# Attention and a mixture of experts on one core: the fills between the first 40 dispatch scatters write 560 elements instead of 200

## The chip, the core and the metric

The kernel runs on one core of one Trainium2 chip, in one launch. The metric is the device time of an execution in microseconds, lower being better. The kernel before has a median of 341.74 us over three runs (339.79, 341.74 and 344.94 us).

## What is computed

The input x has 8 batches of 512 rows of 128 numbers, all float32. The layer is causal attention with one head, a layer norm, a mixture of 8 experts of which each row takes 2, and two more layer norms. Cut to what matters:

```python
x = layernorm(x + softmax(mask(x Wq (x Wk)^T / sqrt(128))) (x Wv))
logits = (x @ gate_w + gate_b) / 0.9
keep = the two largest of the 8 logits of each row
gate = softmax of those two
h = gelu(x @ w1[e] + b1[e])            # 128 -> 512, for each kept expert e
y = sum over the two e of gate[e] * (h @ w2[e] + b2[e])
out = layernorm(x + (layernorm(y) * ln_g + ln_b))
```

## The kernel before

The work is cut into tiles of 128 rows: 4 tiles (TB) a batch, 32 in all. It has two stages that overlap a little.

**Attention and routing** go batch by batch (B = 8). In `step(b)` of each engine, TensorE transposes the next batch's rows, multiplies, transposes the probabilities and weighs the values; VectorE takes the row maxima (`maxima`, L732), adds the residual (L742) and computes the norms; ScalarE takes the exponentials and copies results out of the accumulators (among them v, L586). Two batches behind, VectorE turns the two chosen experts of each row into a place in a table in HBM: `route_link`, whose last link (L840) increments `dispatch_ready`. After the fifth batch, `table_link` also computes which expert each tile of the table belongs to. The table is divided into two groups of batches, `GROUPS = (5, 3)`, and each group's part by expert.

**Dispatch.** GpSimd writes each batch's rows to their places: 8 indirect DMAs (scatters) a batch, one for each of its 4 tiles and each of the 2 choices, 128 rows of 130 numbers each (L1129). Ahead of each scatter stands a fill, `pause(n)` (L1122): GpSimd writes zeros to a tile on one partition that nobody reads, and waits for its own semaphore `paused` before it goes on. There are 64 scatters, 40 of them for the first five batches. Only when all scatters of a group have landed (`dispatched[g]`) may SyncE load tiles of that group: for group 0 this wait stands in SyncE's order behind the copies of rows of batches 0 to 6 (L247) and the fill of the pads (L250), and ahead of the first loads of slots (L276).

**Experts.** 78 tiles of 128 table rows (J = 47 + 31), in loops of 8. For each tile SyncE loads the slots, TensorE transposes them (L510), VectorE copies the transposed tile out (`copy_slots`, L918), TensorE multiplies with the expert's first matrix (L525), ScalarE applies gelu (L668) and copies the expert's weights for a later tile (L661), TensorE multiplies with the second matrix (L536), VectorE weighs the result (L926), and GpSimd scatters it back to row order (`give_back`, L1136), again with a fill ahead of it (for all but the last four). TensorE holds three tiles between a tile's first and second product (LAG = 3).

The last batch's norm and routing stand in VectorE's order ahead of its first `copy_slots`; the places of batch 6 are computed just behind the first two copies, and those of batch 7 within the first eight tiles (at s = 5 and 6). GpSimd's order is: dispatch of batches 0 to 6, three returned tiles, dispatch of batch 7, the other returns. When the returns are in, the last layer norms follow by VectorE and ScalarE.

The order of every engine is written out by hand; no scheduler decides it. Waits are on semaphores alone.

Of the kernel before, what the change touches and what calls it, by code (L numbers as in the profile page):

```python
# [16 lines left out]
GROUPS = (5, 3)  # L17
# [1 line left out]
LAG = 3  # L19
W1_LAG = 3  # L20
AHEAD = 2
PAUSE = 200
TEMPERATURE = 0.9
EPS = 1e-5
BSCALE = 64.0
# [4 lines left out]
def moe_block(nc, emb, W_Q, W_K, W_V, gate_w, gate_b, w1, b1, w2, b2, ln_g, ln_b, out):  # L30
    B, S, D = emb.shape
    E, _, F = w1.shape
    TB = S // P
# [3 lines left out]
    TOPK = 2  # L37
# [25 lines left out]
    with ctx:  # L63
        def sb(name, shape, dt=F32):
            return ctx.enter_context(nc.sbuf_tensor(name, shape, dt))

        def sem(name):
            return ctx.enter_context(nc.semaphore(name))
# [5 lines left out]
        ones_h = sb("ones_h", [P, P], F16)  # L74
        ones = sb("ones", [P, E])
        unused = sb("unused", [P, 1])
        pause_out = sb("pause_out", [1, PAUSE])
        expert_id = sb("expert_id", [P, E])
        first_place = sb("first_place", [P, G, E])
        tile_start = sb("tile_start", [1, MOST_TILES])  # L80
# [996 lines left out]
        def _(pool):  # L1077
            made = sem("made")
            paused = sem("paused")
            g_ = nc.gpsimd  # L1080
# [36 lines left out]

            RETURNS_AHEAD = 3

            def pause(n):  # L1120

                g_.memset(pause_out[:], 0.0).then_inc(paused, 1)  # L1122
                pool.wait_ge(paused, n)

            def dispatch(b, t):
                for k in range(TOPK):
                    pause((b * TB + t) * TOPK + k + 1 + (RETURNS_AHEAD if b == B - 1 else 0))
                    c = k * TB + t
                    g_.indirect_dma_start(slots, bass.IndirectOffsetOnAxis(ap=slot_of[:, b, c:c + 1], axis=0),  # L1129
                                          rows[:, k, b * TB + t, :], None).then_inc(dispatched[0 if b < group_b0[1] else 1], 16)  # L1130

            def give_back(j):
                if j < J - 4:
                    pause(NT * TOPK + j + 1 if j >= RETURNS_AHEAD else NT * TOPK - TB * TOPK + j + 1)
                pool.wait_ge(y_ready, j + 1)
                g_.indirect_dma_start(returned, bass.IndirectOffsetOnAxis(ap=slot_back[:, j:j + 1], axis=0),  # L1136
                                      y[:, j % Y_RING, :], None).then_inc(y_returned[j % Y_RING], 16)
# [6 lines left out]
            for b in range(B):  # L1144
                if b == B - 1:
                    for j in range(RETURNS_AHEAD):
                        give_back(j)
                pool.wait_ge(dispatch_ready, b + 1)
                pool.wait_ge(rows_copied[b], 16)
                for t in range(TB):  # L1150
                    dispatch(b, t)
# [29 lines left out]
```

## Time and profile before

| | |
|---|---|
| median of three runs | 341.74 us (339.79 to 344.94) |
| the profiled execution's own time | 345.1 us |
| its span, first to last instruction | 343.2 us |
| TensorE busy | 264.2 us, 77% |
| VectorE busy | 184.4 us, 54% |
| ScalarE busy | 196.4 us, 57% |
| GpSimd busy | 185.3 us, 54% |
| granted TensorE clock, mean | 0.899 of full speed |
| fills of 200 elements (L1122) | 138, 254 ns each |
| dispatch scatters (L1129) | 64, 976 ns each |
| return scatters (L1136) | 78, 976 ns each |

Busy shares are averages over stages that are limited by different things, so they say little about a change in one stage. The chain of waits follows the work that ended last back to what released it at each step; "issue" is time in which an engine waited for nothing that the profile shows, and "another core or an unknown queue" or "remote" is a wait whose end cannot be matched with the end of an instruction. The timeline gives for each instruction its start, how long it took, how long its engine stood idle before it and what ended that. GpSimd is POOL there, VectorE DVE, ScalarE ACT, TensorE PE (matmuls) and PEld (loads of weights), SyncE SP.

### The profile page before, as it was taken

Reading aid. Unit: us, or ns where it says so; the run is one execution under the profiler, and the core shown is the slowest. Engines: PE = TensorE matmul, PEld = TensorE weight load, DVE = VectorE, ACT = ScalarE, POOL = GpSimd, SP = SyncE. Lnnn points to the kernel's source line nnn. Section 1 sums busy time; section 2 is a strip of 40 time slices with the busy share of each in tenths; the row PEclk is TensorE's granted clock in tenths of the full one; section 3 lists DMA queues with packets and bytes.
Section 4 is the critical chain, followed back from the end, with each engine's and each line's share of the span. In section 5 each row is a group of like instructions: output and inputs, shape, how many; then the busy total and the mean of one; then the engine's idle time right before and its main releaser. Section 6 shows DMA issues by size and latency. Waiting matters only on the chain.

```text
span 343.2 us, 8076 instructions
## 1 busy us (share of the span) xinstructions
PE 264.2 (77%) x1993; PEld 234.2 (68%) x1994; DVE 184.4 (54%) x990; ACT 196.4 (57%) x579; POOL 185.3 (54%) x310
## 2 busy tenths in 40 slices
PE   3998887796863658787799999999999999950000
PEld 2567666485643557686799999999999999950000
DVE  0225783756766643332343333466348878862785
ACT  3357663474533454643568787755555688854251
POOL 8200078766884668678755565656556546560200
PEclk9999999699995869997699999999999999995555
DMA  5996022121232343232212324667699565017403
GB/s 140 273 332 165 8 64 79 39 71 39 72 100 71 76 119 81 56 78 55 64 56 81 96 78 125 179 182 216 193 357 317 179 176 164 31 40 205 140 0 93
DMA packets 45634, 41.94 MB, mean 122 GB/s; under 512 B 5520, under 2 KB 36416, under 8 KB 45600
## 3 DMA queue, kind: packets, MB, share of 16 engines
q1 hardware_dynamic: 41056, 32.20, 33.4%
q0 software_dynamic: 4544, 9.38, 8.0%
q14 instruction: 24, 0.20, 0.2%
q8 instruction: 10, 0.16, 0.2%
HBM read 26.00 MB, written 13.47 MB: 115 GB/s over the span
## 4 chain that ended last, share of the span: by engine, by line
PE 49%; DVE 22%; issue 7%; another core or an unknown queue 7%; DVEq 5%; ACT 5%; DMA 2%; POOL 1%; SPq 1%; ACTq 0%
PE bank L536 15%; PE bank L525 13%; PE bank L425 4%; PE bank L398 4%; DVE sum_stats L931 3%; PE bank L384 2%; DVEq L973 2%; DVE negmax L732 2%; PE bank L389 2%; PE bank L510 2%; PE bank L413 2%; DVE x L926 2%; DVE slot_xT L918 1%; PE bank L533 1%
## 5 line engine op out<-in xcount | busy, mean ns | idle before, releaser
L668 ACT ACTIVATE h<-bank,b_cols 128x128 f32<-128x128 f32 x312 | 89.5, 373 | 51.6 <-PE bank L525 36.7
L1136 POOL DMA_INDIRECT returned<-x,slot_back x78 | 76.1, 976 | 61.8 <-DVE x L926 34.6
L536 PE MATMUL bank<-w_all,h 128*128 x624 | 90.6, 289 | 0.8 <-issue 0.7
L525 PE MATMUL bank<-slot_xT,w_now 128*128 128x128 f32 x624 | 86.0, 282 | 3.3 <-ACT h L668 2.0
L525 PEld LDWEIGHTS bank<-slot_xT,w_now 128*128 128x128 f32 x624 | 79.1, 198 | 4.7 <-issue 3.4
L536 PEld LDWEIGHTS bank<-w_all,h 128*128 128x128 f32 x624 | 78.4, 197 | 2.1 <-issue 1.0
L1129 POOL DMA_INDIRECT slots<-rows,slot_of x64 | 62.5, 976 | 17.8 <-issue 13.9
L1122 POOL MEMSET pause_out<- 1x200 f32 x138 | 35.1, 254 | 44.8 <-DVE rows L840 44.2
L926 DVE TENSOR_SCALAR x<-bank,slot_gate 128x128 f32<-128x128 f32 x78 | 27.1, 348 | 42.7 <-PE bank L536 23.0
L678 ACT ACTIVATE pair<-pair,sum_shift,sum_rstd 128x128 f32<-128x128 f32 x60 | 25.2, 492 | 22.8 <-DVE sum_shift L949 18.8
L661 ACT ACTIVATE w_now<-w_all 128x512 f32 x40 | 26.0, 651 | 7.5 <-issue 7.5
L916 DVE CAST slot_back<-slot_x 128x1 uint32<-128x1 f32 x78 | 11.7, 149 | 32.8 <-PE bank L510 22.4
L732 DVE TENSOR_REDUCE negmax<-bank 128x1 f32<-128x128 f32 (+3 forms) x32 | 15.0, 489 | 24.1 <-PE bank L399 18.6
L425 PE MATMUL bank<-v,probsT 128*128 128x128 f32 x160 | 24.6, 297 | 3.9 <-ACT probsT L595 2.7
L510 PE MATMUL bank<-ident,slot_x 128*128 128x128 f32 x78 | 22.3, 286 | 6.0 <-DVE slot_xT L918 4.0
L425 PEld LDWEIGHTS bank<-v,probsT 128*128 128x128 f32 x160 | 21.4, 205 | 6.2 <-ACT probsT L595 4.4
L608 ACT ACTIVATE probs<-bank,negmax 128x128 f32<-128x128 f32 (+3 forms) x32 | 16.6, 525 | 11.5 <-DVE negmax L732 8.2
L398 PE MATMUL bank<-xT,gT 128*128 128x128 f32 (+3 forms) x64 | 22.6, 477 | 0.0
L595 ACT ACTIVATE probsT<-bank 128x384 f32<-128x384 f32 (+1 forms) x24 | 12.0, 528 | 18.0 <-PE bank L413 13.7
L918 DVE COPY slot_xT<-bank 128x128 f32<-128x128 f32 x78 | 21.9, 281 | 0.0
L533 PE MATMUL bank<-bias,by_expert 128*128 128x128 f16 x78 | 17.3, 222 | 4.8 <-DVE x L926 2.7
L510 PEld LDWEIGHTS bank<-ident,slot_x 128*128 128x128 f32 x78 | 11.5, 148 | 7.5 <-issue 5.9
(135 smaller groups left out, 320.1 us busy)
## 6 DMA issues: line engine op xcount, KB each, us to landing
w_now<-in_L_ffn_w_dram SPq DMA_DIRECT2D x38, 256.0 KB
slot_x<-slots SPq DMA_DIRECT2D x78, 65.0 KB
w_all<-in_L_ffn_w_dram SPq DMA_DIRECT2D x16, 256.0 KB, 5.2
pair<-returned SPq DMA_DIRECT2D x4, 640.0 KB
x<-n_L_attn_embeddings_dram SPq DMA_DIRECT2D x8, 256.0 KB, 4.1
rows<-rows SPq DMA_DIRECT2D x8, 256.0 KB, 2.7
pair<-returned SPq DMA_DIRECT2D x4, 384.0 KB, 4.8
out_dram<-pair SPq DMA_DIRECT2D x2, 640.0 KB, 8.1
```

The source lines that it names most:

```text
L398: nc.tensor.matmul(score[i], gT[:, i * P:(i + 1) * P], xT[:, 0:(i + 1) * P], start=True, stop=False)
L425: m = nc.tensor.matmul(O[:, i * P:(i + 1) * P], probsT[:, o:o + P], v[:, j, :], start=(j == 0), stop=(j == i))
L510: nc.tensor.transpose(psT[s % 2][:, 0:P], slot_x[:, s, 0:D], ident[:]).then_inc(slotT_psum, 1)
L525: m = nc.tensor.matmul(o, w1_now[:, s, cols], slot_xT[:, s % RING, :], start=True, stop=True)
L536: m = nc.tensor.matmul(o, h[:, s % RING, c * P:(c + 1) * P], w2_c, start=False, stop=(c == FC - 1))
L661: nc.scalar.activation(w1_now[:, s % UNROLL, :], w1_all[:, bass.ds(e, 1), :].rearrange("p a f -> p (a f)"), ACT.Copy).then_inc(w1_ready, 1)
L668: m = nc.scalar.activation(h[:, s % RING, cols], psH[s][:, cols], ACT.Gelu, bias=b1_cols[:, c:][:, bass.ds(first, 1)])
L918: vec.tensor_copy(slot_xT[:, s % RING, :], psT[s % 2][:, 0:P]).then_inc(slotT_ready, 1)
L926: vec.tensor_scalar(y[:, j % Y_RING, :], psY[s % 2][:, 0:D], slot_gate[:, s:s + 1], None, ALU.mult).then_inc(y_ready, 1)
L1122: g_.memset(pause_out[:], 0.0).then_inc(paused, 1)
L1129: g_.indirect_dma_start(slots, bass.IndirectOffsetOnAxis(ap=slot_of[:, b, c:c + 1], axis=0), rows[:, k, b * TB + t, :], None).then_inc(dis ...
L1136: g_.indirect_dma_start(returned, bass.IndirectOffsetOnAxis(ap=slot_back[:, j:j + 1], axis=0), y[:, j % Y_RING, :], None).then_inc(y_retur ...
```

## The change

The fill gets a length. Ahead of the scatters of batches 0 to 4 (`b < GROUPS[0]`, 40 fills) it writes 560 elements instead of 200; ahead of the 24 scatters of batches 5 to 7 and ahead of the returns it writes 200 as before. The tile that is filled grows from 200 to 560 elements on its one partition. No instruction is added, removed or moved on any engine, and no wait changes.

```diff
-PAUSE = 200
+PAUSE, LONG_PAUSE = 200, 560
...
-        pause_out = sb("pause_out", [1, PAUSE])
+        pause_out = sb("pause_out", [1, LONG_PAUSE])
...
-            def pause(n):
-
-                g_.memset(pause_out[:], 0.0).then_inc(paused, 1)
+            def pause(n, length=PAUSE):
+
+                g_.memset(pause_out[:, 0:length], 0.0).then_inc(paused, 1)
                 pool.wait_ge(paused, n)

             def dispatch(b, t):
                 for k in range(TOPK):
-                    pause((b * TB + t) * TOPK + k + 1 + (RETURNS_AHEAD if b == B - 1 else 0))
+                    pause((b * TB + t) * TOPK + k + 1 + (RETURNS_AHEAD if b == B - 1 else 0),
+                          LONG_PAUSE if b < GROUPS[0] else PAUSE)
                     c = k * TB + t
                     g_.indirect_dma_start(slots, bass.IndirectOffsetOnAxis(ap=slot_of[:, b, c:c + 1], axis=0),
```

## Rows read from the trace of the kernel before

**Rows 1.** The page's first line: span and instructions.

```profile
span 343.2 us, 8076 instructions
```

**Rows 2.** Busy time by stretch: us, engines with instruction counts, clock, DMA share, GB/s.

```profile
35.80:47.00 11.20, 10.28 (x75) 7.94 (x75) 9.12 (x55) 7.38 (x21) 2.52 (x4) 1.00 0.10 30
47.00:61.90 14.90, 11.83 (x85) 9.04 (x84) 8.22 (x51) 7.30 (x21) 12.11 (x21) 1.00 0.20 64
61.90:75.60 13.70, 11.47 (x64) 8.30 (x64) 8.41 (x52) 7.99 (x22) 9.65 (x17) 0.75 0.19 59
75.60:88.60 13.00, 10.34 (x76) 8.00 (x75) 8.27 (x52) 7.56 (x21) 9.31 (x16) 1.00 0.18 57
88.60:105.90 17.30, 11.45 (x80) 8.81 (x80) 11.62 (x65) 7.28 (x21) 14.17 (x23) 0.93 0.31 93
...
168.50:304.00 135.50, 135.22 (x1166) 131.62 (x1166) 79.61 (x391) 97.43 (x315) 80.53 (x130) 0.99 0.52 156
```

**Rows 3.** The chain of waits, in order of time: start, us, what.

```profile
55.71 3.14 another core or an unknown queue
...
101.28 3.08 another core or an unknown queue
...
132.56 5.38 another core or an unknown queue
```

**Rows 4.** Timeline, copy of v: start, us, instruction, [idle before, releaser].

```profile
42.92 1.06 PE L389 MATMUL bank<-wv,xT 128*128 128x128 f32 x8
44.02 0.60 ACT L586 ACTIVATE v<-bank 128x512 f32<-128x512 f32 x1 [0.61 <-PE bank L389]
...
55.78 0.50 PE L389 MATMUL bank<-wv,xT 128*128 128x128 f32 x3
...
58.87 0.60 ACT L586 ACTIVATE v<-bank 128x512 f32<-128x512 f32 x1 [3.16 <-remote]
```

**Rows 5.** Timeline of GpSimd: fills and scatters where its trains begin and end.

```profile
43.88 0.25 POOL L1122 MEMSET pause_out<- 1x200 f32 x1 [32.94 <-DVE rows L840]
...
70.02 0.26 POOL L1122 MEMSET pause_out<- 1x200 f32 x1 [1.82 <-DVE rows L840]
...
83.56 0.25 POOL L1122 MEMSET pause_out<- 1x200 f32 x1 [1.47 <-DVE rows L840]
...
106.75 0.97 POOL L1129 DMA_INDIRECT slots<-rows,slot_of  x1 [0.28 <-issue]
...
144.74 0.98 POOL L1136 DMA_INDIRECT returned<-x,slot_back  x1 [1.66 <-DVE x L926]
```

**Rows 6.** GpSimd's groups by shape: instruction, count, busy us, mean ns, idle before.

```profile
L1122 POOL MEMSET pause_out<- 1x200 f32 x138 | 35.1, 254 | 44.8 <-DVE rows L840 44.2 <-issue 0.4
L1106 POOL MEMSET empty<- 128x3900 f32 x1 | 3.3, 3337 | 0.0
```

**Rows 7.** Timeline, the first expert tile, all engines.

```profile
117.40 1.97 SPq L276 DMA_DIRECT2D slot_x<-slots  x3
...
119.87 0.78 PE L510 MATMUL bank<-ident,slot_x 128*128 128x128 f32 x2 [1.91 <-DMA slot_x<-slots]
...
123.65 0.28 DVE L918 COPY slot_xT<-bank 128x128 f32<-128x128 f32 x1
...
124.32 1.95 PE L525 MATMUL bank<-slot_xT,w_now 128*128 128x128 f32 x8
...
127.33 0.86 ACT L668 ACTIVATE h<-bank,b_cols 128x128 f32<-128x128 f32 x3
```

**Rows 8.** Timeline of VectorE: weighed results of expert tiles 0 and 10.

```profile
135.73 0.35 DVE L926 TENSOR_SCALAR x<-bank,slot_gate 128x128 f32<-128x128 f32 x1 [1.41 <-PE bank L536]
...
168.48 0.33 DVE L926 TENSOR_SCALAR x<-bank,slot_gate 128x128 f32<-128x128 f32 x1
```

**Rows 9.** Timeline of GpSimd: one return in the steady stage.

```profile
180.75 0.97 POOL L1136 DMA_INDIRECT returned<-x,slot_back  x1 [0.78 <-POOL pause_out L1122]
```

**Rows 10.** Line L789: count, duration ns min/median/max, first and last start, forms.

```profile
L789 DVE TENSOR_SCALAR var<-moments x8: 169/170/324, 27.7 to 119.0; 128x4 f32<-128x4 f32 x8
```

## The prediction, written before the changed kernel had run

> **What bounds the kernel now.** I read the page first: the profiled execution has a span of 343.2 us [rows 1] and took 345.1 us as a whole. That is 3.4 us above the median of the three timed runs (341.74) and at the top of what they show (339.79 to 344.94). I then cut the span into stages [rows 2]. From 168.5 us on TensorE is busy 135.22 of 135.50 us and nothing of this change lies there: one tile of the expert stage takes 2.0 us, as GpSimd's giving back of each tile shows (0.25 + 0.78 + 0.97 us) [rows 9]. All that can move lies ahead of it. There the attention batches should be read one by one. The stretch 35.80 to 47.00 is a step of attention, with its routing, that ran almost without GpSimd beside it: 11.2 us. The same step takes 14.9, 13.7 and 13.0 us in the next three stretches, in which GpSimd is busy 9 to 12 us, and 17.3 us in the fourth. TensorE has not got more to do in them (10.3 to 11.8 us); it and the others wait.
>
> What they wait for is told by the chain of waits: pieces of 3.14 and 3.08 us named "another core or an unknown queue" in attention and one of 5.38 us, the first of its kind there, in the expert stage [rows 3]. The timeline says what such a piece is. TensorE's last matmul of v ended at 55.78 + 0.50 = 56.28 us, and ScalarE, which waits for it alone, began at 58.87, 2.6 us later. The same hand-over one step earlier (the matmuls ended at 42.92 + 1.06 = 43.98) took 0.04 us: ScalarE began at 44.02 [rows 4]. So news from TensorE arrives late, by some microseconds, while GpSimd runs its scatters without a break. It is not late from the start. A train of scatters began at 43.88 and the first hand-overs in it were punctual; a second began at 70.02, a third at 83.56 [rows 5]. The step that follows each break begins punctually and the next one is late again (13.0 us for the step that holds the break of 1.47 us, then 17.3). It looks like something that fills a little in each cycle of fill and scatter, and that a break of 1.5 to 1.8 us empties.
>
> **The change: the fill.** A cycle is fill, semaphore and scatter, 0.25 + 0.28 + 0.97 = 1.51 us unrounded (the 16 of the train from 83.56 begin 0.53 us into it and at 106.75: 22.66/15 = 1.511) [rows 5]. What a fill of 560 elements takes no row shows, but two others give the price of an element: 3900 a partition take 3337 ns and 200 take 254 ns, so 3083/3700 = 0.833 ns each [rows 6]. 360 more elements are 0.30 us, the fill 0.55 us, and the cycle 1.81 us. 40 fills of the 138 change: 40 × 0.30 = 12.0 us more on GpSimd.
>
> **What that puts on the path.** The scatters of batches 0 to 4 begin at 43.88 as before, since nothing ahead of them changes. At 1.81 us they no longer catch up with routing, so there are no breaks: the 40th ends at 43.88 + 40 × 1.807 = 116.2 us, where it ended at 106.75 + 0.97 = 107.7. SyncE waits for all 40 before it loads the first tile's slots. It issued that load at 117.40 [rows 7], so it was not waiting for the scatters then; now it will. From the end of the last scatter to the load I take 2.0 us for landing and 1.0 us for reading the addresses. Neither is in a row; the bounds are zero, and 2.5 us for the landing, which is what the slot load takes from its issue at 117.40 to the transpose that waits for it at 119.87. So the load goes out at 119.2 (117.4 to 120), the transpose follows at 121.7, and VectorE's copy of the transposed tile, the gate of the expert stage, at about 122.3 (120.5 to 123.5).
>
> **What it takes off the path.** If the cycle of 1.81 us ends the late news in attention, the three steps of 14.9, 13.7 and 13.0 us become 11.2 each (8.0 us less), and the one of 17.3 us becomes 11.2 + 3.35, the additional VectorE time of the tile table (11.62 − 8.27) [rows 2]: 2.7 us less. 10.7 us together. VectorE's copy, which came at 123.65 because VectorE was still at the last batch's routing, could come at 113.0. The scatters then gate it, at 122.3. So of 10.7 us only 1.4 are left at this point. A little more is left at the first activation: at 127.33 ScalarE was behind with the last batch's rows and its table; with those done early it starts when the eight matmuls end, 122.3 + 0.67 + 1.95 = 124.9, 2.4 us earlier [rows 7].
>
> **Whether the cycle suffices.** Bounds: the fill may not help at all (excess per cycle over 0.30 us), or end it entirely. The nearest rows: a break of 1.47 us emptied what the eight scatters from 70.02 had filled, 0.18 us per cycle at most, and the break of 1.82 us what 16 had, 0.11 us. 0.30 is more than both. From the other side, cycles of 2.0 us go on for 130 us with TensorE busy throughout [rows 2, 9]. 1.81 is nearer to 2.0 than to 1.51. I take it that it suffices, with some 7 in 10.
> The Trainium skill, "TensorE: Matmul & The Clock Gate", section "The cost: per-tile semaphore tail", says that TensorE's increments serialize at about 26 ns each, with no part for GpSimd in it. By it the 2.6 us of [rows 4] would have another cause, attention would stay as slow as it is and the time would be that of the third rival below. The trace disagrees with it as the whole price.
>
> **What the longer fill costs beside it.** VectorE's tensor_scalar on the variances takes 170 ns as a rule and 324 ns at its longest [rows 10]. If that was a fill in its way, and each such operation can be held up by one for up to its length, 0.55 instead of 0.25 us, then with about 5 of them in a step and a fill present in 0.55/1.81 = 31% of the time, this is 5 × 0.31 × 0.28 = 0.4 us a step, 2 us in five steps. Hidden: attention has 122.3 − 113.0 = 9 us of room. Without that cover it would count whole. The Trainium skill, "SBUF — State Buffer", section "Who interferes with whom", has the rule: the two engines share a port pair that one holds for a whole instruction; by it too it is this hidden cost and no more.
>
> **What is given back.** Batches 5 to 7 keep their fill of 200. Their 24 scatters and the first three returns of tiles had breaks in them, one of 1.66 us before the return at 144.74 [rows 5]; now batches 5 and 6 follow the 40 without a break from 116.2, until 128.2 and 140.3. The cycle of 1.51 us is there when the experts start, so the late news can fall on the very first tiles; in the trace of before its first piece is at 132.56 [rows 3], 5 us after the first activation. Tiles 0 to 10 left VectorE from 135.73 to 168.48, 3.3 us each instead of 2.0 [rows 8], and this ended when GpSimd had worked off its backlog. That point hangs on GpSimd's own work: 116.2 + 24 × 1.507 + 10 × 1.507 = 167.4, the same within about 1 us as before. Tiles done by then: about as many. I put the loss at +1 to +3 us, 1.9 taken, so that the head start of 2.4 us is nearly gone: −0.5 us net. 345.1 − 0.5 = 344.6 for an execution like the profiled one, and 341.2 against the median. Since the profiled run is the slowest of the kind, the median one probably had less late news to lose, which argues against counting on more.
>
> **Rivals.**
> (1) *The cycle is still too short, or the longer one is worse.* With 40 scatters and no break, no step after the third is relieved: 47.0 + 3 × 14.9 + 17.3 = 109.0 instead of 105.9, and the last step another 3.7 us longer: +6.8 us at most, 348.5; +4 to +5 where it is partly relieved. It decides if the excess of a cycle is over 0.30 us. For it: all three breaks go, and they are what emptied it so far. Against: the two quotients above. Slower than before.
> (2) *The expert stage gains too.* If the train from 116.2 starts empty and the breaks fall well, the stage from 135.7 to 168.5, where ten tiles took 32.8 us and at 2.0 us each would take 20, gives back a part: half of 12.8 plus the head start is −9 us, 333; a quarter is −5.6, 336. For it: the head start is there and it is a large pool. Against: those scatters' cycle is untouched.
> (3) *The late news has nothing to do with the fill's length.* Attention stays, the copy comes at 123.65 as before or a little later, the slot load is 1.8 us later but still ahead of it: +0.5, 342.
>
> **How the numbers follow.** The forecast (attention relieved, gain absorbed, −3 to +2.5 us around 341.2) gets 0.50; rival 1 0.14; rival 2 0.21; rival 3 0.15. About 2% (6.8 us) is what a measurement of this kernel can tell from no change. Faster by more than that is half of rival 2 and a little of the forecast's edge: 0.13. Slower by more is rival 1 at its full price: 0.08. The rest, 0.79, is within it. The range reaches to a quarter of rival 2's pool below and to nearly the full price of rival 1 above: 335 to 347.5.
>
> **What would show it.** Fills of 560 at 0.55 us and a cycle of 1.81; the 40th scatter ending near 116.2 with no break between batches; steps of 11.2 us between the largest row maxima, and ScalarE's copy of v within 0.1 us of the last matmul; VectorE's first slot copy near 122.3, waiting for the load and no longer for its own routing; pieces of several us with no named releaser from 125 to 168. It is wrong if those pieces stay ahead of 116 us (rival 1 or 3), or if tile 10 leaves VectorE well ahead of 165 us (rival 2).

## The result: 1.5% slower on the first chip, with attention relieved as forecast

In the first comparison the changed kernel takes 346.96 us (median of 4, 346.06 to 347.98), the kernel before 342.82 us (4 runs, 339.79 to 344.94): ratio 1.0146, 95% interval [1.0079, 1.0213]. That is +4.1 us. The forecast was 341.2 us, or 0.5 us less than the kernel before, the range 335 to 347.5, with 0.79 on "within 2%". (The median of the kernel before is 342.82 here and 341.74 in the prediction because a fourth run, 343.9 us, was added.) The measured time lies inside the range, but the direction is the other one, beyond the interval of the measurement.

The profiled executions are 345.1 us before and 347.31 us after; they are 2.2 us apart, and their spans, from first to last instruction, 2.3 us (343.2 and 345.5). The other 1.9 us is how far the two profiled runs stand from their medians: the one of before is 2.3 us slower than its median, the one of after 0.35. So the traces can account for 2.3 us and no more.

From the profile of the changed kernel, first its span, then the fills in their two lengths (GpSimd's groups by shape: count, busy us, mean ns, idle before):

```profile
span 345.5 us, 8076 instructions
```

```profile
L1122 POOL MEMSET pause_out<- 1x200 f32 x98 | 24.9, 254 | 2.2 <-DVE rows L840 2.1
L1122 POOL MEMSET pause_out<- 1x560 f32 x40 | 22.2, 554 | 33.6 <-DVE rows L840 33.6
```

A fill of 560 takes 554 ns, as worked out from [rows 6]. The steps of attention, busy time by stretch in the columns of [rows 2]:

```profile
35.80:47.00 11.20, 10.28 (x75) 7.94 (x74) 9.13 (x56) 7.37 (x22) 2.16 (x3) 1.00 0.08 24
47.00:58.30 11.30, 10.32 (x75) 7.99 (x74) 8.38 (x52) 7.42 (x22) 9.35 (x14) 1.00 0.21 67
58.30:69.50 11.20, 10.26 (x74) 7.94 (x73) 8.12 (x52) 7.35 (x22) 9.53 (x13) 1.00 0.20 61
69.50:80.80 11.30, 10.38 (x75) 8.03 (x74) 8.26 (x52) 7.47 (x22) 9.63 (x13) 1.00 0.19 59
80.80:95.50 14.70, 11.75 (x84) 8.99 (x82) 12.27 (x66) 7.31 (x21) 12.47 (x17) 1.00 0.19 60
117.20:127.10 9.90, 3.27 (x17) 2.68 (x18) 0.84 (x7) 0.03 (x1) 7.95 (x15) 0.50 0.52 133
```

Where [rows 2] had 14.9, 13.7, 13.0 and 17.3 us stand 11.3, 11.2, 11.3 and 14.7: attention is 10.4 us further at 95.5 us. These stretches are not quite the steps. The largest row maxima, which part the steps in [rows 2], begin at 47.65, 58.95, 70.20, 81.43 and 95.50 in this trace, since attention as a whole began 0.65 us later in it. From one to the next the steps are 11.3, 11.3, 11.2 and 14.1 us, 11.0 us less in sum. The hand-over of v to ScalarE, late by 2.6 us in [rows 4], is prompt with GpSimd working beside it; from the timeline:

```profile
54.87 1.06 PE L389 MATMUL bank<-wv,xT 128*128 128x128 f32 x8
...
55.96 0.60 ACT L586 ACTIVATE v<-bank 128x512 f32<-128x512 f32 x1 [0.61 <-PE bank L389]
```

The matmuls end at 55.93, ScalarE begins at 55.96. What was late in [rows 4] was the news and not TensorE's work: there TensorE went on with its next matmuls while ScalarE waited, from 56.12 us (the ends of matmuls are modelled in the profile):

```profile
56.12 0.60 PE L438 MATMUL bank<-ident,rows 128*128 128x128 f32 x4
```

Then comes the last row of the stretches above: from the end of the 40th scatter at 117.2 us to the first activation of the expert stage TensorE is busy 3.3 of 9.9 us, at half its clock (0.50, the 1.2 GHz level; it had stood idle for 14.9 us before). The clock is no rival for the difference: in the stretch of the first ten tiles it is 0.88 in both traces (123.7 to 168.5 us before, 127.1 to 172.6 now), and its mean over the span 0.899 and 0.898. The timeline of this start, all engines, answers to [rows 5] (last scatter) and [rows 7]:

```profile
116.23 0.97 POOL L1130 DMA_INDIRECT slots<-rows,slot_of  x1 [0.28 <-POOL pause_out L1122]
...
119.70 4.07 SPq L276 DMA_DIRECT2D slot_x<-slots  x8
...
122.02 0.45 PE L510 MATMUL bank<-ident,slot_x 128*128 128x128 f32 x1 [14.93 <-DMA slot_x<-slots]
...
122.64 0.28 DVE L918 COPY slot_xT<-bank 128x128 f32<-128x128 f32 x1
...
124.75 0.45 PE L510 MATMUL bank<-ident,slot_x 128*128 128x128 f32 x1 [1.24 <-DVE slot_xT L918]
...
124.99 1.94 PE L525 MATMUL bank<-slot_xT,w_now 128*128 128x128 f32 x8
...
127.07 1.14 ACT L668 ACTIVATE h<-bank,b_cols 128x128 f32<-128x128 f32 x4 [11.53 <-issue]
```

So 10.4 us of relief arrive as 0.3: the first activation is at 127.07, where [rows 7] had 127.33. The third transpose (L510) stands in TensorE's order ahead of the first tile's products, and it did not wait for slots or for VectorE: its slots had landed by 122.94 and VectorE's first copy was done. Between the second transpose and the third TensorE's sequencer reads the numbers of the next tiles' experts (`expert_numbers`, L540), the first time from 123.03 to 124.59 us; the transpose followed at once. In the kernel before it did so from 120.31 to 121.83, while TensorE waited for VectorE's routing, so it cost nothing there. All readings of that line, before and changed (count, duration ns min/median/max, first and last start):

```profile
L540 PEldq TENSOR_LOAD <-expert_of x11: 785/1323/1519, 120.3 to 300.5; - x11
L540 PEldq TENSOR_LOAD <-expert_of x11: 783/1317/1555, 123.0 to 303.4; - x11
```

Now the chain of waits runs over the scatters, the landing of the last one, SyncE's reading of the tiles' addresses (L259) and the landing of the second tile's slots:

```profile
115.40 0.56 POOL pause_out L1122
...
116.23 2.32 DMA slots<-rows,slot_of
118.57 0.54 SPq L259
...
120.30 2.69 DMA slot_x<-slots
...
132.40 4.82 another core or an unknown queue
```

The last of these rows is late news again, right at the first tiles. VectorE's weighed results of tiles 0 and 10, as in [rows 8]:

```profile
140.24 0.35 DVE L926 TENSOR_SCALAR x<-bank,slot_gate 128x128 f32<-128x128 f32 x1 [0.31 <-remote]
...
172.61 0.35 DVE L926 TENSOR_SCALAR x<-bank,slot_gate 128x128 f32<-128x128 f32 x1 [1.94 <-PE bank L536]
```

From first activation to tile 0 it takes 13.2 us, before 8.4; to tile 10 45.5, before 41.2: the kernel has lost 4.4 us here, all of it by tile 0. Part of it comes back up to tile 16, which leaves VectorE at 184.45 against 181.64, and the distance of 2.8 us then stays to the last tile. Of the 4.4 us 3.1 are left there.

Below, "late news" in us is a sum over the semaphore updates of TensorE that came more than 0.15 us behind the latest instruction that could have made them; where several updates of one semaphore are outstanding this counts too little, and it is a measure of how much is late, not of time lost. In the kernel before it was 62.5 us in 28 updates between 44 and 117 us, in the changed one none there, and 39.8 us in 11 updates between 117 and 150 (before 23.7 in 11).

The late updates do not come at any time. In the trace of before the one that ends the wait of [rows 4] came at 58.73 us and the next at 59.49, 60.26, 61.01 and 61.76, 0.75 us apart, which is half of GpSimd's cycle of 1.51 us. Of the 33 late ones between 44 and 200 us that came within such a cycle, 17 came 0.6 to 0.7 us after the start of its scatter and 13 came 1.3 to 1.5 us after it; the punctual ones are spread over the cycle. It looks as if updates queue and are let through twice in a cycle of GpSimd. That fits the prediction's picture of something that fills and is emptied by a break; what it is no trace shows.

### The profile page after: what moved, and what is told of

Same layout as the page of the kernel before. It is cut to its first block, busy times and chain, and to the rows that moved or that the text cites. A ratio compares the mean times of both kernels' runs of the same rounds, so it can differ in the third digit from the quotient of the medians.

```text
span 345.5 us, 8076 instructions
## 1 busy us (share of the span) xinstructions
PE 261.1 (76%) x1993; PEld 233.5 (68%) x1994; DVE 184.5 (53%) x990; ACT 195.9 (57%) x579; POOL 197.5 (57%) x310
## 4 chain that ended last, share of the span: by engine, by line
PE 53%; POOL 18%; DVE 9%; issue 8%; DMA 4%; another core or an unknown queue 2%; ACT 2%; DVEq 2%; SPq 1%; ACTq 0%; POOLq 0%
PE bank L536 21%; PE bank L525 20%; POOL slots L1130 11%; POOL pause_out L1122 7%; PE bank L510 3%; PE bank L398 2%; PE bank L533 2%; PE bank L425 1%; PE bank L384 1%; DVE sum_stats L931 1%; PE bank L389 1%; DMA pair<-returned 1%; DVE sum_tmp L751 1%; DMA slot_x<-slots 1%
## 5 line engine op out<-in xcount | busy, mean ns | idle before, releaser
L525 PE MATMUL bank<-slot_xT,w_now 128*128 128x128 f32 x624 | 87.0, 284 | 4.7 <-ACT h L668 2.6
L536 PE MATMUL bank<-w_all,h 128*128 x624 | 89.6, 288 | 0.8 <-issue 0.8
L525 PEld LDWEIGHTS bank<-slot_xT,w_now 128*128 128x128 f32 x624 | 79.9, 200 | 5.8 <-issue 3.5
L1130 POOL DMA_INDIRECT slots<-rows,slot_of x64 | 62.7, 979 | 17.8 <-POOL pause_out L1122 12.5
L1122 POOL MEMSET pause_out<- 1x200 f32 (+1 forms) x138 | 47.1, 341 | 35.9 <-DVE rows L840 35.7
L510 PE MATMUL bank<-ident,slot_x 128*128 128x128 f32 x78 | 22.7, 291 | 16.8 <-DMA slot_x<-slots 15.5
L608 ACT ACTIVATE probs<-bank,negmax 128x128 f32<-128x128 f32 (+3 forms) x32 | 16.6, 525 | 14.1 <-DVE negmax L732 12.9
L510 PEld LDWEIGHTS bank<-ident,slot_x 128*128 128x128 f32 x78 | 11.6, 148 | 18.7 <-issue 17.1
L533 PE MATMUL bank<-bias,by_expert 128*128 128x128 f16 x78 | 17.3, 222 | 4.0 <-DVE x L926 2.0
L595 ACT ACTIVATE probsT<-bank 128x384 f32<-128x384 f32 (+1 forms) x24 | 11.7, 530 | 12.5 <-PE bank L413 10.8
```

The source lines that it names most:

```text
L510: nc.tensor.transpose(psT[s % 2][:, 0:P], slot_x[:, s, 0:D], ident[:]).then_inc(slotT_psum, 1)
L525: m = nc.tensor.matmul(o, w1_now[:, s, cols], slot_xT[:, s % RING, :], start=True, stop=True)
L536: m = nc.tensor.matmul(o, h[:, s % RING, c * P:(c + 1) * P], w2_c, start=False, stop=(c == FC - 1))
L1122: g_.memset(pause_out[:, 0:length], 0.0).then_inc(paused, 1)
```

## The experiments

Theory A: a cycle of fill and scatter of 1.51 us makes TensorE's news late, a longer one does not; the expert stage starts when the 40th scatter has landed, and meets a train of scatters at 1.51 us without a break. Theories B, C and D stand in the expectations. The kernel before took 342.8 us in the first comparison, 333.2 beside the first four experiments and 316.0 to 316.1 beside all later ones. The record gives the latter two different chips and names none for the first comparison; by its time it is called the first chip here, the others the second and the third. Each experiment is compared with runs of the kernel before on its own chip, and only so. The times in the expectations of the first four experiments and of the first ones on the third chip were worked out from another chip's and have to be read as distances to the kernel before.

### On the second chip (kernel before 333.17 us, median of 7)

**All 64 fills at 560.**

```diff
-                          LONG_PAUSE if b < GROUPS[0] else PAUSE)
+                          LONG_PAUSE)
```

> All 64 dispatch scatters get the fill of 560 elements, the returns keep 200. Theory A (a cycle of 1.51 us of fill and scatter makes TensorE's semaphore news late, one of 1.81 us does not; the change lost its gain because batches 5 and 6 now run at 1.51 us just as the experts start): no late news until the returns after batch 7; tile 0 leaves VectorE near 131 instead of 140.2, tile 10 near 155 instead of 172.6, although the 64th scatter ends some 7 us later; 335 to 342 us, faster than the changed kernel (346.96). Theory B (the loss is only that the 40 scatters, and GpSimd's work behind them, end later): another 24 x 0.30 = 7.2 us on GpSimd make it 350 or more.

Measured: 341.48 us, ratio 1.0259 [1.0203, 1.0315], 8.3 us over the kernel before. The late news in front of tile 0 is gone as theory A says, but as a distance the time is theory B's (7 or more over the kernel before) and not theory A's (1 to 8 us under it). Whether it is faster than the changed kernel is not known, as that one was not run on this chip.

**560 only for batches 5 to 7 (200 for the first 40).**

```diff
-                          LONG_PAUSE if b < GROUPS[0] else PAUSE)
+                          LONG_PAUSE if b >= GROUPS[0] else PAUSE)
```

> The fills of batches 0 to 4 are 200 elements as in the kernel before, those of batches 5 to 7 are 560. Theory A: attention steps stay at 13 to 17 us with late news, the expert stage's first ten tiles lose little: tile 0 near 132, tile 10 near 155 to 160; 332 to 338 us against 342.8 before. Theory B: 24 x 0.30 us more on GpSimd behind an unchanged start: 343 to 348.

Measured: 329.55 us, ratio 0.9896 [0.9842, 0.995], 3.6 us less than before where theory A had 5 to 11 less and theory B 0 to 5 more. The two runs differ in the first 40 fills alone, and 560 there costs 11.9 us (341.48 − 329.55). In both the first tiles meet little late news (2.1 and 4.1 us between 117 and 150), and the first activations are 4.7 us apart, at 126.1 and 121.39. The traces do not give the whole 11.9: their spans are 6.9 us apart (339.7 and 332.8), since the profiled run of the second was 5.0 us above its own median (334.55) and does not stand for it. In the first of the two the tiles follow from the start at the pace of 2.0 us (timeline of VectorE, tiles 0, 3 and 7):

```profile
133.13 0.34 DVE L926 TENSOR_SCALAR x<-bank,slot_gate 128x128 f32<-128x128 f32 x1
...
137.88 0.35 DVE L926 TENSOR_SCALAR x<-bank,slot_gate 128x128 f32<-128x128 f32 x1 [0.59 <-PE bank L536]
...
146.23 0.35 DVE L926 TENSOR_SCALAR x<-bank,slot_gate 128x128 f32<-128x128 f32 x1 [0.59 <-PE bank L536]
```

Tile 0 leaves 7.0 us behind the first activation (126.1). Late news from 117 to 150 us: 2.1 us. Then GpSimd works its backlog off at 1.51 us a cycle and the news is late from 150 to 200: 38.7 us, and 49.3 in the trace of 560 for batches 5 to 7 (on the first chip the changed kernel had 25.4 there and the kernel before 20.0). So late news is moved more than removed: the backlog has to be worked off at some time, and that is done with the fill of 200.

**380 instead of 560.**

```diff
-PAUSE, LONG_PAUSE = 200, 560
+PAUSE, LONG_PAUSE = 200, 380
```

> As the changed kernel, but the long fill is 380 elements: cycle 1.66 us, the 40th scatter ends near 110.5 instead of 117.2. Theory A: 0.15 us more per cycle than in the kernel before is at the edge; if it is enough, attention steps are 11.2 us and the first slot load goes out near 113.5, 6 us before that of the changed kernel, and most of it survives: 340 to 343 us. If it is not enough, steps of 13 to 15 us are back and the time is 343 to 346. Theory B (only the end of the 40 scatters counts): 341.

Measured: 338.19 us, ratio 1.0146 [1.0074, 1.0219], 5.0 us over the kernel before, where the expectation had it up to 3 us faster; the 40th scatter ended at 111.7. The steps were 11.3, 11.2, 11.3 and 13.7 us, no late news at all in attention: 0.15 us more per cycle suffice on this chip. Still no gain: the experts' first activation (121.4) meets the train at 1.51 us and the late news of 117 to 150 is 28.4 us. Tile 0 came 8.5 us behind the first activation and tile 10 38.3 (7.0 and 26.1 with all 64 fills at 560).

**The changed kernel with a rest ahead of batches 5 and 6.** The expectation has 2.5 us for each rest. The three fills are back to back without scatters, 1.8 us in the trace (0.61 each), so GpSimd has 3.7 us more to do and not 5.0.

```diff
             def dispatch(b, t):
+                if b in (5, 6) and t == 0:
+                    for r in range(3):
+                        g_.memset(pause_out[:], 0.0).then_inc(rested, 1)
+                        pool.wait_ge(rested, (5, 6).index(b) * 3 + r + 1)
```

> The changed kernel with three more fills of 560 elements (2.5 us of rest) ahead of batch 5's first scatter and three ahead of batch 6's: it gives back the breaks that the kernel before had there. Theory A: news from TensorE is punctual for the first expert tiles; tile 0 leaves VectorE near 135 to 137 instead of 140.2; 344 to 346 us although GpSimd has 5.0 us more to do. Theory B: up to 5 us slower, 349 to 352.

Measured: 346.46 us, ratio 1.041 [1.0353, 1.0466]. Tile 0 left 134.85, 7.2 us behind the first activation (127.64):

```profile
127.64 1.14 ACT L668 ACTIVATE h<-bank,b_cols 128x128 f32<-128x128 f32 x4 [12.14 <-PE bank L525]
...
134.85 0.34 DVE L926 TENSOR_SCALAR x<-bank,slot_gate 128x128 f32<-128x128 f32 x1
```

Tile 0 is as theory A says, and the news is late further on: 18.5 us between 117 and 150, 37.8 between 150 and 200, and tile 10 came 40.9 us behind the first activation. The total is 13.3 us over the kernel before, where theory A had +1 to +3 and theory B +6 to +9, so this run confirms neither. All in all theory A is right on this chip on where the news is late, and its times were too low in all four runs; there was less to win in attention (38.3 us of late news with fills of 200, in the trace of 560 for batches 5 to 7, where the first chip had 62.5). The changed kernel itself was not run on this chip, so how much the breaks win or lose here is not known.

### On the third chip (kernel before 316.04 to 316.11 us)

**The kernel before and the changed one, for their traces.**

> The kernel before, unchanged, for a trace on the same chip as the next three. The late news in attention should be less than in the first trace, where it added up to 11 us: the end of the 40th scatter and the first slot load some 3 to 5 us earlier than 107.7 and 117.4, tile 0 leaving VectorE near 130. 331 to 334 us.

> The changed kernel, unchanged, on that chip. Theory A (the start of the expert stage is set by the end of the 40th scatter, 117.2 us whatever attention does, and the scatters of batches 5 and 6 at 1.51 us a cycle make news late there): first slot load at 119.7 again, attention steps 11.2 us, 343 to 347 us; more than the 1.5% over the kernel before of the first comparison, since there is less to win in attention here. If the loss had its cause in the expert stage alone, the distance to the kernel before would be the same 4 us, 337.

> The kernel before, for its trace beside the next three. The three chips so far differ: the same program took 342.8, 333.2 and 316.1 us, with 62, some 38 and 0 us of late news from TensorE in attention. Theory A: the time and the late news go together again, with the 40th scatter ending between 104 and 108 us.

> The changed kernel. Theory A (the end of the 40th scatter at 117 us sets the start of the expert stage whatever attention does): no late news in attention on any chip, first activation at 126 to 127.6 us; slower than the kernel before by 1 to 2% where that has much late news in attention, by 3.5% where it has none. Rival: a fixed price of the longer fills would give the same distance on every chip.

> The kernel before, for its trace beside the next three. If this chip shows late news it takes over 330 us and its 40th scatter ends later than 104.2; if not, 315 to 317.

> The changed kernel. With late news on this chip: attention without it, first activation 126 to 127.6 us, and 11 to 13 us from there to tile 0's result; 1 to 3% slower. Without late news: 7.3 us from the one to the other, 3.6 to 4% slower, as twice before.

Before: 315.17, 315.64 and 316.63 us. The expectation of 331 to 334 was wrong, since the chip was another. Changed: 327.81, 329.12 and 328.29 us, ratios 1.0362 [1.0314, 1.041], 1.04 [1.0358, 1.0443] and 1.0384 [1.0331, 1.0437]. The same program is 27 us faster than on the first chip, and the profile says by what: no update of TensorE is more than 0.15 us late in it, and its tile 10 leaves VectorE 27.8 us earlier (140.7 and 168.5), while from there to the last tile both take 137 to 138 us. (The "some 38" us that the expectation gives for the second chip are those of the run with 560 for batches 5 to 7; the kernel before has no trace there.) Stretches of the kernel before on this chip, in the columns of [rows 2]:

```profile
47.00:58.30 11.30, 10.38 (x76) 8.04 (x75) 8.27 (x52) 7.47 (x21) 9.07 (x17) 1.00 0.23 71
58.30:69.50 11.20, 10.22 (x74) 7.88 (x73) 8.17 (x52) 7.31 (x21) 9.25 (x15) 1.00 0.21 67
69.50:80.80 11.30, 10.32 (x75) 7.99 (x75) 8.21 (x52) 7.41 (x21) 9.07 (x17) 1.00 0.22 70
114.10:140.70 26.60, 26.60 (x228) 26.18 (x228) 13.59 (x91) 21.18 (x67) 21.78 (x36) 0.95 0.35 85
```

With fills of 200 the steps take 11.2 to 11.3 us, and ten expert tiles 19 us. The start of the expert stage there, all engines:

```profile
107.32 3.54 SPq L276 DMA_DIRECT2D slot_x<-slots  x7
...
109.84 0.66 PE L510 MATMUL bank<-ident,slot_x 128*128 128x128 f32 x2 [4.08 <-DMA slot_x<-slots]
...
110.46 0.28 DVE L918 COPY slot_xT<-bank 128x128 f32<-128x128 f32 x1
...
114.08 1.14 ACT L668 ACTIVATE h<-bank,b_cols 128x128 f32<-128x128 f32 x4
...
121.59 0.34 DVE L926 TENSOR_SCALAR x<-bank,slot_gate 128x128 f32<-128x128 f32 x1
```

And in the changed kernel on the same chip:

```profile
119.44 4.08 SPq L276 DMA_DIRECT2D slot_x<-slots  x8
...
122.44 0.28 DVE L918 COPY slot_xT<-bank 128x128 f32<-128x128 f32 x1
...
126.62 1.14 ACT L668 ACTIVATE h<-bank,b_cols 128x128 f32<-128x128 f32 x4 [11.71 <-PE bank L525]
...
133.95 0.34 DVE L926 TENSOR_SCALAR x<-bank,slot_gate 128x128 f32<-128x128 f32 x1
```

The first load is 12.1 us later, the first activation 12.5, tile 0 12.4, the span 12.8 us (313.4 and 326.2). Little else changes: where there is no late news, the change costs the whole delay of the 40th scatter. The rival of a fixed price on every chip is out: it is 4.1 us on the first chip (interval 2.7 to 7.3) and 11.7 to 13.1 us on this one.

**A rest instead of longer fills.** The kernel before, with

```diff
             def dispatch(b, t):
+                if b == 4 and t == 0:
+                    for r in range(22):
+                        g_.memset(pause_out[:], 0.0).then_inc(rested, 1)
+                        pool.wait_ge(rested, r + 1)
```

> The kernel before, all fills at 200, with 22 more fills of 200 elements (some 11 us of rest) ahead of the first scatter of batch 4, so that the 40th scatter ends near 116 as in the changed kernel, with no longer fill anywhere. Theory A: the end of the 40th scatter is what costs, so this costs like the changed kernel: first slot load near 118 to 119, 342 to 347 us. Theory C (the longer fills cost through what they do beside VectorE, port or otherwise): as the kernel before plus at most what the first load is later, 335 to 338, well under the changed kernel.

Measured: 323.29 us, ratio 1.0215 [1.0169, 1.0262]. The 22 fills took 6.8 us, not 11 (0.31 each), so the 40th scatter ended at 111.6, 7.4 us later than in the kernel before. The time in theory A's expectation was taken from another chip and means nothing; the claim in it holds: the last expert tile leaves VectorE at 285.4, 7.6 us later than before, with no longer fill anywhere. Theory C is out as the main cause.

**280 ahead of the first 40, 380 ahead of the other 24**, twice, and beside the second of them **the changed kernel with the two rests** (the edit shown for the second chip; the last expectation of the three is for it).

```diff
-PAUSE, LONG_PAUSE = 200, 560
+PAUSE, LONG_PAUSE = 200, 380
...
-                          LONG_PAUSE if b < GROUPS[0] else PAUSE)
+                          280 if b < GROUPS[0] else LONG_PAUSE)
```

> Fills of 280 elements (cycle 1.57 us) ahead of the first 40 scatters, 380 (1.66 us) ahead of the 24 of batches 5 to 7, returns 200. Theory A: the 40th scatter ends by 108 to 110, the slot load follows by 111 to 113, little late news in attention and in the expert stage before the returns: 325 to 330 us, faster than before (333). If 280 is too short to matter: as the run with 560 on batches 5 to 7 alone, 329.5.

> 280 elements ahead of the first 40 scatters, 380 ahead of the other 24. With late news: 40th scatter at 107, little late news ahead of the returns, 3 to 8 us faster than the kernel before. Without: 2.5 us slower, as once before.

> The changed kernel with 2.5 us of rest ahead of batch 5 and ahead of batch 6. Theory D (the missing breaks cost the 5 us between first activation and tile 0's result): with late news, 7.2 us between the two instead of 11 to 13, but the news is late further on, since GpSimd has 5 us more to work off, and the time is within 3 us of the changed kernel. Without late news: as the changed kernel within 1 us, for GpSimd's 5 us more is hidden behind tiles of 2.0 us.

Measured: 318.33 and 318.67 us, ratios 1.0071 [1.0043, 1.0098] and 1.0085 [1.0056, 1.0114]: slower here by 0.7 and 0.9%, as the second expectation says for a chip without late news (the first, of 325 to 330 us against 333, was for another chip and would have been a gain). The rests: 328.39 us, 1.0386 [1.0345, 1.0428], with the changed kernel at 328.29 beside it: 3.7 us more on GpSimd behind the 40th scatter (1.8 us for each rest here too) are hidden.

**20 ahead of the first 40 (200 for the rest)**, and **380 only for batches 5 to 7**. Their edits, in this order:

```diff
-PAUSE, LONG_PAUSE = 200, 560
+PAUSE, LONG_PAUSE = 200, 20
...
-        pause_out = sb("pause_out", [1, LONG_PAUSE])
+        pause_out = sb("pause_out", [1, PAUSE])
```

```diff
-PAUSE, LONG_PAUSE = 200, 560
+PAUSE, LONG_PAUSE = 200, 380
...
-                          LONG_PAUSE if b < GROUPS[0] else PAUSE)
+                          LONG_PAUSE if b >= GROUPS[0] else PAUSE)
```

> Fills of 20 elements instead of 200 ahead of the first 40 scatters (some 105 ns, a cycle of 1.36 us). Theory A: on a chip with late news it grows in attention and the time rises by 3 to 10 us over the kernel before; on a chip without, the 40th scatter ends at 98 to 100 us but VectorE's routing of the last batch ends at 110 as before, so the time is that of the kernel before within 1 us, though a cycle this short may bring late news there too.

> 200 elements ahead of the first 40 scatters as before, 380 ahead of the 24 of batches 5 to 7. Theory A: the start of the expert stage is that of the kernel before; with late news it wins some 4 us or more in the first ten tiles (560 there won 3.6 us on a chip with a medium amount); without late news nothing to win, and GpSimd's 3.6 us more is hidden, 0 to +1 us.

Measured: 314.75 us, ratio 0.9961 [0.9939, 0.9984], and 316.87 us, ratio 1.0015 [0.9993, 1.0036]. At a cycle of 1.36 us there is no late news on this chip either. The 40th scatter ends at 99.8, 4.4 us earlier than before, and the last tile leaves VectorE at 278.3 as before: there the chain of waits runs through VectorE's routing of the last batch, which ends at 111.4, and the scatters have no price.

The runs of this chip side by side, by the 40th scatter's end, the weighed result of the last expert tile, and the median:

| | 40th scatter ends | last tile | median us |
|---|---|---|---|
| 20 elements | 99.8 | 278.3 | 314.75 |
| before (three traces) | 104.2 to 104.9 | 277.8 to 278.6 | 316.1 |
| 200 / 380 | 105.6 | 279.7 | 316.87 |
| 280 / 380 (first) | 106.8 | 280.5 | 318.33 |
| 280 / 380 (second) | 108.5 | 281.5 | 318.67 |
| before with a rest | 111.6 | 285.4 | 323.29 |
| changed with the two rests | 116.8 | 291.2 | 328.39 |
| changed (three traces) | 116.9 to 117.5 | 290.2 to 290.8 | 327.8 to 329.1 |

From 104.2 to 117.0 the last tile is later by 12.4 us: 0.97 us for each us, whether a longer fill or a rest makes the scatters late. Below 104 it is flat, by the one run that is there.

## Why the prediction went wrong, step by step

- **The fill and its cycle**: right. 554 ns and 1.81 us; the 40th scatter ended at 117.2 instead of 116.2. The 1.0 us is a train that began 0.65 us later (44.53), a first scatter that took 0.18 us longer than the others, as in the kernel before, and one cycle that was 0.24 us longer.
- **The cycle suffices to end the late news in attention**: right; 11.0 us less in the four steps, 10.7 forecast. With 380 elements, 0.15 us more per cycle, it still sufficed on the second chip, which fits the break-even of at most 0.18 us worked out from the breaks. Why a longer cycle suffices no run shows.
- **The start then hangs on the scatters**: right. The first load went out at 119.70 (119.2), VectorE's copy was at 122.64 (122.3). The two terms that stood in no row came out at 2.5 us in sum instead of 3.0: the last scatter had landed 2.32 us after its start, which is 1.35 us after its end (2.0 taken), and the load followed 1.15 us later (1.0 taken).
- **A head start of 2.4 us at the first activation**: wrong, it was 0.3. This is the step that cost most in the traces, 2.1 us. The term 0.67 + 1.95 between copy and activation measured 2.35 + 1.94, and 0.14 to the activation. The 0.67 was read from a start in which the slots had long been there and TensorE had read the experts' numbers while it waited. With the load on the path the second transpose came 1.0 us behind the first (122.02 and 123.04), and the reading of the experts' numbers, 1.56 us from 123.03, which the sum did not have, held the third transpose until 124.75 and the first products until 124.99. In no trace here is the first activation less than 3.5 us behind the first copy; the sum had 2.6.
- **A loss of 1 to 3 us, 1.9 taken, in the first ten tiles**: wrong in size, 4.4 us at tile 10, of which 3.1 stay to the last tile. The text saw that the breaks go and that the train of 1.51 us meets the first tiles, and then let the catching-up of GpSimd set the price. It held that GpSimd would be level with the tiles at 167.4 and "tiles done by then: about as many"; in fact two fewer were done (tile 8 left at 168.49, where tile 10 had left at 168.48). On tile 0 alone the price was 4.8 us (13.2 instead of 8.4). That late news is what it paid for is supported by the second chip, where tile 0 came 8.5 us behind the first activation with the train of 1.51 us ahead of it, and 7.0 and 7.2 without the train or with breaks in it, and by the third, where without late news it takes 7.0 to 7.5 us in the traces of either kernel.
- **−0.5 us against the profiled run**: +2.2 measured there (345.1 to 347.31). The 2.7 us between (2.8 by the spans) are the two steps above, 2.1 and 1.2 us, less 0.5 that comes back behind the last tile. **Carried over to the median** without change: +4.1, another 1.9 us. The text said that a slow profiled run has more late news to lose than the median one and gave it no number. No trace of a run at the median shows whether that is the reason; the interval of the comparison, 2.7 to 7.3 us, begins close to the 2.2 of the traces. What the other chips show is that the gain depends on how much late news there is, and the delay of the scatters does not. With none, the same change costs 12 us.
- **Rival 1** (slower, since the cycle is too short) named the right side for a wrong reason (attention was relieved in full). No rival had the start of the expert stage as a price in itself: the 9.5 us by which the 40th scatter ends later were set against the last batch's routing, at 123.65. On the first chip this cover held, with the copy 1.0 us earlier than before; but it was itself made of late news, and on the third chip, where the copy of the kernel before is at 110.46, it is gone.
- **The rule of the Trainium skill**, "TensorE: Matmul & The Clock Gate", "The cost: per-tile semaphore tail", some 26 ns for an increment: on the third chip no update of TensorE is over 0.15 us late, which does not speak against it; on the first one hand-over took 2.6 us, a hundred times as much, and with the longer fill 0.03 us. So the rival by which the fill's length has nothing to do with it (rival 3) is out.
- **The port shared by VectorE and GpSimd** (the Trainium skill, "SBUF — State Buffer", "Who interferes with whom"): the operation at L789, 324 ns at its longest in [rows 10], took 609 ns once beside a longer fill:

```profile
L789 DVE TENSOR_SCALAR var<-moments x8: 170/170/609, 28.4 to 108.1; 128x4 f32<-128x4 f32 x8
```

It ran from 108.15 to 108.76 us, and the fill from 108.17 to 108.73; that it ended with the fill fits the rule. The first three of the four steps did not get longer by it: 11.2 to 11.3 us with either fill on the third chip. The fourth, with the tile table, did: 13.45 us with fills of 200 and 14.1 with 560 there, in three traces each. So the 0.4 us for each step were too much for most and too little for that one, and hidden as forecast. That this 0.65 us is the port's is not shown.

**Open.** What makes the news late on one chip and not on another was not found; the durations of the DMAs and of GpSimd's instructions are nearly the same. Whether it is the chip at all is not shown either: the record has one occasion for each of the first two and three for the third. How the 4.1 us of the first comparison divide into the start and the first tiles is read from that comparison's two traces alone: the changed kernel with and without its rests was put side by side only on the third chip, which has no late news. The kernel before has no trace on the second chip. No version is shown better than the kernel before on every chip: 560 elements for batches 5 to 7 alone won 1.0% on the second chip (0.5 to 1.6%); 380 there cost nothing measurable on the third. 560 there was not tried on the third, nor 380 on the second.

## What to carry to other kernels

A relief upstream is worth only what the next gate lets through: before slowing one engine to unblock others, work out when its own last result is due with the disturbance gone, not beside the disturbed times of the others. A cover that consists of a disturbance is not a cover, and it may be absent on the next chip. The same holds inside the gate: a time read between two instructions that both waited for something else is no price for the stretch between them, since what ran hidden behind the wait (here TensorE's reading of the experts' numbers) comes onto the path when the wait goes. And a train of short scatters that falls on the first tiles of a stage has its price there, 4.8 us on tile 0 in the first comparison; breaks ahead of them helped tile 0 and did not shorten the whole.

## What the runs showed of the hardware

The same program took 342.8, 333.2 and 316.1 us in comparisons on what the record has as at least two chips. The difference between the first and the last goes with the time at which TensorE's semaphore updates arrive while GpSimd issues indirect DMAs every 1.51 us: up to 4.9 us late in attention on the first chip, never over 0.15 us on the third, not even at 1.36 us a cycle. Between 44 and 200 us only TensorE's updates are late in the first trace; one of VectorE's came 0.35 us late, none of ScalarE's or GpSimd's. The late ones arrive at two points of GpSimd's cycle, 0.75 us apart (30 of 33 in the first trace). A cycle longer by 0.30 us on the first chip and by 0.15 us on the second had no late update in attention, and in the first trace none was late for 7 us behind the break of 1.82 us and for 11 us behind the one of 1.47 us. GpSimd's fills on one partition took 104 ns for 20 elements, 254 for 200 and 554 for 560. TensorE's sequencer took 0.8 to 1.7 us to read the numbers of the next experts, and in the changed kernel the transpose behind the first reading began 0.13 us after its end.
